# The front of a graph kernel rebuilt: part of VectorE's preparation goes to GpSimd

## The chip, the cores and the metric

The kernel runs on one core of one Trainium2 chip. The metric is the device time of one execution in microseconds. A profile of one execution, with its own time, stands beside the times; times of the trace count from its first instruction.

## The reference, cut to what matters

Two graph layers over 1,250 nodes with 512 features and 21,250 edges. The first is an attention layer, the second a mixture of four expert networks, which this change doesn't touch.

```python
h = jnp.maximum(_layernorm(x), 0.0)
# first layer, nodes = h
h = nodes @ W + b_w
s_dst = h @ a[:D_OUT]; s_src = h @ a[D_OUT:]
e = leaky_relu(s_dst[dst] + s_src[src] + b_a, 0.2)
w = exp(e); alpha = w / segment_sum(w, dst)[dst]
out = segment_sum(alpha[:, None] * h[src], dst)
x = x + out
# second layer: x = x + top-2 mixture of 4 experts, each two mean-aggregating layers
```

## The kernel before, in words

**Front.** The edges come as 170 chunks of 125. TensorE makes, in 22 blocks of up to 8 chunks (`hot_block`, L1811), values that are positive only where an edge's source has the right place within its tile; ScalarE (L794) or VectorE (L1189, block 2 only, `HOT_DVE`) turns them into 0 or 1 while moving them out of PSUM (`hot_columns`). Three pairs of PSUM banks take turns, so block u waits for the eviction of block u - 3. Between the blocks TensorE does small jobs for the table that says which chunks belong to which window of 25 destination nodes (`spread_spans`, `turn_edges`, `sum_tables`, `turn_tables`); VectorE works the table out and signals `tab_ready`. VectorE also takes the statistics of the ten tiles of x (`row_stats`), and ScalarE the square root (`std_ready`); `scales` makes rstd and shift, with which ScalarE normalises tile 0 (`norm`).

**Batches.** Ten batches, b = 0 to 9, each for one tile of 125 nodes and five windows. VectorE makes 25 one-hots for the destinations (L1301). TensorE transposes the normalised tile (L1898), makes 25 counting matmuls (L1860) into CT, then the scores (`scores`, L1879 and L1882, h with the vectors W a) and the product h W (L1923 to L1925). For precision h and W are split in a high and a low part: hT_hi, hT_lo, W0_hi, W0_lo. ScalarE copies high parts (`turned_high0`, `product_high`), the bias into PSUM (`bias_in`) and the counts out (`windows_out`); VectorE makes the low parts (`turned_low0` L1285, `product_low` L1281).

**W and a.** The scores need W a for both halves of a: `source_vectors` (L1184), eight VectorE instructions that multiply 128 x 512 of W with a and sum along the row; two more do the bias (L1260). `first_weights_low` is W0_lo = W - W0_hi (L1270). All of that stands in VectorE's order between batch 0's one-hots and batch 1's. GpSimd (POOL) has made constants and issued three small loads (a_b, bw_b, ba_c) and then waits until the batches are over.

Every engine works through its own list in order, with semaphores between them; in a name of a signal, `x_ready(n)` is a wait for the n-th signal x. `link` makes an engine wait for its own instruction.

## Time and profile before

| | us |
|---|---|
| median of 3 runs | 745.5 (745.43 to 745.51) |
| the profiled execution | 744.08 |
| its span, first to last instruction | 742.3 |
| TensorE busy | 717.8 (97%) |
| VectorE busy | 428.0 (58%) |
| ScalarE busy | 398.1 (54%) |
| GpSimd busy | 184.1 (25%) |

The span is what the trace covers; 1.8 us of the execution's time lie around it. Matmuls are pipelined and their ends are modelled, so busy TensorE is not TensorE at its peak; spans on GpSimd are rough. A group's line gives busy time, the mean of one instruction, and then the idle time before the group.

### The profile page before, as it was taken

Reading aid. Unit: us, or ns where it says so; the run is one execution under the profiler, and the core shown is the slowest. Engines: PE = TensorE matmul, PEld = TensorE weight load, DVE = VectorE, ACT = ScalarE, POOL = GpSimd, SP = SyncE. Lnnn points to the kernel's source line nnn. Section 1 sums busy time; section 2 is a strip of 40 time slices with the busy share of each in tenths; the row PEclk is TensorE's granted clock in tenths of the full one; section 3 lists DMA queues with packets and bytes.
Section 4 is the critical chain, followed back from the end, with each engine's and each line's share of the span. In section 5 each row is a group of like instructions: output and inputs, shape, how many; then the busy total and the mean of one; then the engine's idle time right before and its main releaser. Section 6 shows DMA issues by size and latency. Waiting matters only on the chain.

```text
span 742.3 us, 12047 instructions
## 1 busy us (share of the span) xinstructions
PE 717.8 (97%) x3574; PEld 582.2 (78%) x3574; DVE 428.0 (58%) x1056; ACT 398.1 (54%) x897; POOL 184.1 (25%) x204
## 2 busy tenths in 40 slices
PE   5899999999999999999999999999999999999994
PEld 3589977888888888777777777878888888888883
DVE  8899889999752538622722622657444544444341
ACT  6966769677653521511511511347677667767751
POOL 4000000000000100850300010045666555655511
PEclk9999999999999999999999999999999999999998
DMA  9100000111501247799699695379844994438950
GB/s 207 39 4 3 4 3 18 53 35 35 165 8 58 79 123 240 217 333 326 228 354 328 200 359 197 99 184 264 300 93 88 264 343 120 86 69 225 290 156 6
DMA packets 46444, 115.19 MB, mean 155 GB/s; under 512 B 8340, under 2 KB 8552, under 8 KB 46361
## 3 DMA queue, kind: packets, MB, share of 16 engines
q1 hardware_dynamic: 28581, 77.60, 32.7%
q0 software_dynamic: 9136, 19.65, 11.6%
q10 hardware_dynamic: 8644, 16.86, 6.9%
q8 instruction: 48, 0.79, 0.4%
q14 instruction: 35, 0.29, 0.1%
HBM read 64.89 MB, written 50.08 MB: 155 GB/s over the span
## 4 chain that ended last, share of the span: by engine, by line
PE 92%; DVE 4%; ACT 1%; issue 1%; POOL 0%; DVEq 0%; ACTq 0%; POOLq 0%
PE ps L1783 16%; PE ps L1784 16%; PE ps L1785 16%; PE ps L2185 7%; PE ps L2184 6%; PE ps L2052 3%; PE ps L2053 3%; PE ps L1985 3%; PE ps L1860 3%; PE ps L1979 3%; PE ps L1980 3%; PE ps L2115 2%; PE ps L1923 1%; PE ps L1811 1%; PE ps L1925 1%; PE ps L1924 1%
## 5 line engine op out<-in xcount | busy, mean ns | idle before, releaser
L1110 ACT ACTIVATE agn<-ps,rec 32x128 f32<-32x128 f32 x336 | 120.7, 359 | 38.7 <-PE ps L2185 34.8
L1044 ACT ACTIVATE slots<-he_t 125x512 fp32r<-125x512 f32 x40 | 25.3, 635 | 150.9 <-DVE he_t L1581 146.6
L2185 PE MATMUL ps<-slots,CTs 125*128 x230 | 89.9, 391 | 0.0
L1581 DVE TENSOR_TENSOR he_t<-ps,b_b 125x512 f32<-125x512 f32 x40 | 27.6, 691 | 105.5 <-PE ps L1785 72.3
L728 POOL DMA_INDIRECT hrow<-t_d,piece_i x80 | 76.1, 951 | 25.7 <-issue 23.5
L2184 PE MATMUL ps<-slots,CTs 125*128 x207 | 80.7, 390 | 0.0
L1746 DVE TENSOR_TENSOR tm<-ps,b_b 128x512 f32<-128x512 f32 x23 | 15.9, 692 | 84.3 <-PE ps L1785 84.2
L1783 PE MATMUL ps<-W,agT_hi 128*125 128x512 f32 x160 | 63.5, 397 | 0.0
L1783 PE MATMUL ps<-W,h2T_hi 128*125 128x512 f32 x160 | 63.4, 396 | 0.0
L1785 PE MATMUL ps<-W,agT_lo 128*125 128x512 f32 x160 | 63.3, 396 | 0.0
L1784 PE MATMUL ps<-W,agT_hi 128*125 128x512 f32 x160 | 63.2, 395 | 0.0
L1784 PE MATMUL ps<-W,h2T_hi 128*125 128x512 f32 x160 | 63.2, 395 | 0.0
L1785 PE MATMUL ps<-W,h2T_lo 128*125 128x512 f32 x160 | 63.1, 394 | 0.0
L733 POOL DMA_INDIRECT out<-tg,rec x23 | 37.0, 1607 | 84.2 <-ACT tg L1099 64.3
L1674 DVE CAST CTs<-ps 125x512 fp32r<-125x512 f16 (+1 forms) x69 | 37.3, 596 | 29.1 <-PE ps L2115 29.1
L1301 DVE TENSOR_SCALAR onehot_g<-iota_h,column 125x250 bf16<-125x250 f16 x250 | 49.7, 282 | 5.9 <-PE ps L1860 4.6
L2185 PEld LDWEIGHTS ps<-slots,CTs 125*128 125x128 f32 x230 | 43.2, 188 | 9.7 <-issue 0.3
L2184 PEld LDWEIGHTS ps<-slots,CTs 125*128 125x128 f32 x207 | 38.9, 188 | 8.2
L1979 PE MATMUL ps<-nat_hi,p_hi 125*125 125x512 f32 x100 | 41.0, 410 | 0.2 <-issue 0.2
L712 POOL DMA_INDIRECT crow<-c_d,rec x23 | 22.7, 988 | 73.4 <-DVE W L1549 66.7
L1783 PE MATMUL ps<-slots,heT 128*128 x92 | 38.2, 415 | 1.7 <-DVE heT L1708 1.7
L1980 PE MATMUL ps<-nat_lo,p_hi 125*125 125x512 f32 x100 | 39.5, 395 | 0.0
(316 smaller groups left out, 1665.4 us busy)
## 6 DMA issues: line engine op xcount, KB each, us to landing
he_d<-slots SPq DMA_DIRECT2D x30, 448.0 KB
slots<-he_d SPq DMA_DIRECT2D x30, 448.0 KB
w_d<-slots SPq DMA_DIRECT2D x3, 4096.0 KB, 18.7
slots<-w_d SPq DMA_DIRECT2D x24, 512.0 KB
t_d<-he_t SPq DMA_DIRECT2D x40, 224.0 KB
raw<-in_L_gnn_Wl ACTq DMA_DIRECT2D x4, 1024.0 KB, 7.2
raw<-in_L_gnn_Wr ACTq DMA_DIRECT2D x4, 1024.0 KB, 5.6
slots<-in_L_gnn_Wl ACTq DMA_DIRECT2D x4, 1024.0 KB, 10.0
```

Source lines behind the costliest of these rows:

```text
L728: g.indirect_dma_start(hrow[i % HB][:, q, :], None, t_d.rearrange("e p t (r f) -> (e p t r) f", r=RQ), bass.IndirectOffsetOnAxis(ap=piece_ ...
L733: g.indirect_dma_start(out, bass.IndirectOffsetOnAxis(ap=i32(rec[:, i, 2:3]), axis=0), tg[i % 3][:], None, bounds_check=N - 1, oob_is_err= ...
L1110: last = a.activation(agn[32 * r:32 * r + 32, q, :], ps[n, 3 + i % 2, 128 * r:128 * r + 128], ACT.Copy, scale=rec[n, i, 4:5])
L1301: last = v.tensor_scalar(onehot_g[:, k, j, :], iota_h[:], column[:, b % 2 * BW + k, j:j + 1], None, ALU.is_equal)
L1674: v.tensor_copy(CTs[:, 4 * r:4 * r + n, :], turned_counts(r, n)).then_inc(cts_ready.sem, 1)
L1783: mm(o, l_hi, r_hi, start=start, stop=False)
L1784: mm(o, l_hi, r_lo, start=False, stop=False)
L1785: return mm(o, l_lo, r_hi, start=False, stop=stop)
L1979: mm(o, p_hi[:, g % RA, m, n], nat_hi[:, s, :], start=s == 0, stop=False)
L1980: mm(o, p_hi[:, g % RA, m, n], nat_lo[:, s, :], start=False, stop=False)
L2184: mm(o, CTs[:, t, :], part(k, P, t * 1024, P), start=False, stop=False)
L2185: last = mm(o, CTs[:, t, :], part(k, P, t * 1024 + D, P), start=False, stop=t == T - 1)
```

## The change

- **GpSimd** (after its constants) waits for the small loads and the edge work, adds the two halves of a, multiplies the bias with them and folds the row once (512 to 256). When W has landed it multiplies all of W (128 x 2,048) with each half of a and folds each product once, then makes W0_lo, then folds the nine rows of 256 to 128 and to 64.
- **VectorE** sums the 64 that are left of each row, at the place after hT_lo of batch 0 and ahead of batch 1's one-hots; its own products of W and its W0_lo go. The statistics move behind the table; the registers of batch 0 are loaded during them; `scales` stands after the first five one-hots.
- **ScalarE** makes W0_hi, the bias copy and norm 0 between the last evictions of the front, and the copies of the table's columns later; it waits for wa before it writes nat_hi 0 and the counts of batch 0 (they lie where GpSimd's tiles are).
- **TensorE** makes 12 matmuls of the identity first (`wake`), the hot blocks have all 128 rows (63 of them zero), the small jobs stand one or two blocks later, VectorE evicts block 3 in place of block 2, and batch 0 sums its product by parts: four with both high parts, four with hT_lo, four with W0_lo, and makes the scores last.

```diff
         e_src = at("e_src", [CR, CG, P], F32, 6016)
         e_t = at("e_t", [CR, CG, P], F32, 9024)
         e_g = at("e_g", [CR, CG, P], F32, 12032)
-        e_q = at("e_q", [2 * CR + 1, CG, P], F32R, 15040)
+        e_q = at("e_q", [128, CG, P], F32R, 15040)
         e_mm = at("e_mm", [CR, 2, CG], F32, 18048)
         e_dg = at("e_dg", [CR, 2 * CG, CR], F32, 18112)
...
-        q_sel = at("q_sel", [2 * CR + 1, CR, P], F32R, R1 + 20480)
+        q_row = at("q_row", [128, P], F32, 21920)
+        q_at = at("q_at", [128, CR], F32, 22432)
+        q_sel = at("q_sel", [128, CR, P], F32R, R1 + 20480)
         a_b = at("a_b", [128, 2, D], F32, R1)
-        spill = [at(f"spill_{k}", [128, D], F32, R1 + 6144 + 2048 * k) for k in range(2)]
+        half = D // 2
+        weighed = at("weighed", [128, KC, D], F32, 0)
+        halves = at("halves", [128, 2 * KC + 1, half], F32, 33408)
+        quarters = at("quarters", [128, 2 * KC + 1, half // 2], F32, 33408 + 4 * (2 * KC + 1) * half)
+        eighths = at("eighths", [128, 2 * KC + 1, half // 4], F32, 0)
+        a_sum = at("a_sum", [P, D], F32, R1 + 6144)
+        assert 33408 + 6 * (2 * KC + 1) * half <= R1
         g_b = at("g_b", [NW, NCH], F32, 28704)
...
         SPREAD, SPREAD_BANKS = (4, 4, 2), (5, 7, 5)
         MAGIC = 12582912.0
         WHOLE = NCH // CR
-        HOT_DVE = (2,)
+        HOT_DVE = (3,)
         HOT_ACT = tuple(u for u in range(NU) if u not in HOT_DVE)
...
             for k in range(2):
                 link(g.affine_select(out=q_at[0:2 * CR, :], in_=q_at[0:2 * CR, :], compare_op=ALU.not_equal, fill=1.0,
                                      base=-CR * k, pattern=[[-1, CR]], channel_multiplier=1))
-            link(g.memset(q_at[2 * CR:, :], 1.0))
+            link(g.memset(q_at[2 * CR:2 * CR + 1, :], 1.0))
...
+
+            def folded(o, i, n):
+                return g.tensor_tensor(o, i[:, :, 0:n], i[:, :, n:2 * n], ALU.add)
+
+            pool.wait_ge(*small_in(48))
+            pool.wait_ge(*rows_ready(1))
+            g.memset(halves[:, 2 * KC, :], 0.0)
+            link(g.tensor_tensor(a_sum[:], a_b[0:P, 0, :], a_b[0:P, 1, :], ALU.add))
+            link(g.tensor_tensor(weighed[0:P, 0, :], bw_b[:], a_sum[:], ALU.mult))
+            link(folded(halves[0:P, 2 * KC:, :], weighed[0:P, 0:1, :], half))
+            pool.wait_ge(*w0_in(16))
+            for w in range(2):
+                link(g.tensor_tensor(weighed[:], W0_f[:], a_b[:, w, :].unsqueeze(1).broadcast_to([128, KC, D]), ALU.mult))
+                link(folded(halves[:, w * KC:(w + 1) * KC, :], weighed[:], half))
+            pool.wait_ge(*w0_hi_ready(1))
+            g.tensor_tensor(W0_lo[:], W0_f[:], f32(W0_hi[:]), ALU.subtract).then_inc(w0_lo_ready.sem, 1)
+            link(folded(quarters[:], halves[:], half // 2))
+            folded(eighths[:], quarters[:], half // 4).then_inc(wa_f_ready.sem, 1)
...
             def product_high(t):
                 act.wait_ge(*hw_done(t + 1))
+                if t == 0:
+                    act.wait_ge(*wa_ready(2))
                 copy(nat_hi[:, t, :], ps[0:P, 6, :]).then_inc(hw_hi_ready.sem, 1)
 
             def turned_high0(b):
                 act.wait_ge(*turned(b + 1))
                 if b > 0:
                     act.wait_ge(*hw_done(b))
+                if b == 1:
+                    act.wait_ge(*s_done(1))
                 copy(hT_hi[:], ps[:, 5, 0:KC * P].rearrange("p (c n) -> p c n", n=P)).then_inc(hT_hi_ready.sem, 1)
 
...
             for u in range(NU):
                 if u in HOT_ACT:
                     hot_columns(u)
-                if u == 3:
+                if u == 5:
                     act.wait_ge(*rows_turned(1))
                     copy(e_gc[:], ps[0:P, 7, 0:CG * CR]).then_inc(cols_ready.sem, 1)
-                if u == 10:
+                if u == 13:
                     act.wait_ge(*tab_ready(1))
                     columns(0)
+                if u == 15:
+                    act.wait_ge(*w0_in(16))
+                    copy(W0_hi[:], W0_f[:]).then_inc(w0_hi_ready.sem, 1)
                 if u == 16:
                     act.wait_ge(*var_ready(1))
                     a.activation(std[:], std[:], ACT.Sqrt).then_inc(std_ready.sem, 1)
-            act.wait_ge(*norm_ready(1))
-            norm(0)
-            act.wait_ge(*w0_in(16))
-            copy(W0_hi[:], W0_f[:]).then_inc(w0_hi_ready.sem, 1)
+                if u == 17:
+                    bias_in(0)
+                if u == 18:
+                    act.wait_ge(*norm_ready(1))
+                    norm(0)
 
             for b in range(T):
                 if b == T - 1:
...
-                bias_in(b)
+                if b > 0:
+                    bias_in(b)
+                if b == 0:
+                    act.wait_ge(*wa_ready(2))
                 if b < T - 1:
                     windows_out(b)
 
             link(v.tensor_copy(q_f[:], q_i[:]))
             v.tensor_scalar(q_row[0:CR, :], q_f[0:CR, :], 2.0, None, ALU.mult)
             v.memset(q_row[CR:2 * CR, :], -1.0)
+            v.memset(q_row[2 * CR:, :], 0.0)
             link(v.tensor_tensor(q_f[2 * CR:, :], q_f[2 * CR:, :], q_f[2 * CR:, :], ALU.mult))
-            link(v.tensor_scalar(q_row[2 * CR:, :], q_f[2 * CR:, :], -1.0, 1.0, ALU.mult, ALU.add))
+            link(v.tensor_scalar(q_row[2 * CR:2 * CR + 1, :], q_f[2 * CR:, :], -1.0, 1.0, ALU.mult, ALU.add))
...
+            def batch_flags(b):
+                more = more_here(dve, b)
+                return more, dve.value_load(tab_b[0:1, b:b + 1, BW + 1:BW + 2], min_val=0, max_val=NW * NG)
+
...
-            dve.wait_ge(*x_in(32))
-            row_stats(range(0, 2))
             hot_columns(HOT_DVE[0])
             dve.wait_ge(*spans_spread(1))
...
-            row_stats(range(2, 4))
+            dve.wait_ge(*x_in(32))
+            row_stats(range(0, 1))
             dve.wait_ge(*n_summed(1))
             v.tensor_copy(tab_f[:, 2:3], ps[0:NW, 7, 0:1]).then_inc(tab_f_ready.sem, 1)
-            row_stats(range(4, T // 2))
+            row_stats(range(1, 2))
             dve.wait_ge(*tab_turned(1))
 
...
+            row_stats(range(2, T // 2))
             dve.wait_ge(*x_late_in(32))
-            link(row_stats(range(T // 2, T)))
+            late = row_stats(range(T // 2, T))
+            dve.wait_ge(*flag_ready(2))
+            dve.wait_ge(*tab_ready(1))
+            first_flags = batch_flags(0)
+            link(late)
             for t in range(T):
                 last = v.bn_aggr(x_mv[:, t, :], x_stats[:, t, :])
...
             def sources():
-                dve.wait_ge(*w0_in(16))
-                dve.wait_ge(*small_in(48))
-                source_vectors(0)
-                source_vectors(1)
-                for w in range(2):
-                    dve.wait_ge(*wa_f_ready(2 * KC - 1 + w))
-                    v.scalar_tensor_tensor(spill[w][0:P, :], bw_b[:], 1.0, a_b[0:P, w, :], ALU.mult, ALU.mult,
-                                           accum_out=ab[:, w:w + 1]).then_inc(ab_ready.sem, 1)
-                dve.wait_ge(*wa_f_ready(2 * KC))
+                dve.wait_ge(*wa_f_ready(1))
+                v.tensor_reduce(ab[:, 0:1], eighths[0:P, 2 * KC, :], AX.X, ALU.add).then_inc(ab_ready.sem, 1)
+                link(v.tensor_reduce(wa_f[:].rearrange("p c w -> p w c"),
+                                     eighths[:, 0:2 * KC, :].rearrange("p (w c) n -> p w c n", w=2), AX.X, ALU.add))
                 link(v.tensor_copy(wa[:, :, 0:2], wa_f[:]))
                 v.tensor_tensor(wa[:, :, 2:4], wa_f[:], f32(wa[:, :, 0:2]), ALU.subtract).then_inc(wa_ready.sem, 1)
-                dve.wait_ge(*ab_ready(2))
-                v.tensor_scalar(s_add[:], ab[:, 0:1], ab[:, 1:2], ba_c[:], ALU.add, ALU.add).then_inc(wa_ready.sem, 1)
-
-            def first_weights_low():
-                dve.wait_ge(*w0_hi_ready(1))
-                v.tensor_tensor(W0_lo[:], W0_f[:], f32(W0_hi[:]), ALU.subtract).then_inc(w0_lo_ready.sem, 1)
+                dve.wait_ge(*ab_ready(1))
+                v.tensor_scalar(s_add[:], ab[:, 0:1], ba_c[:], None, ALU.add).then_inc(wa_ready.sem, 1)
 
...
-                more = more_here(dve, b)
-                before = dve.value_load(tab_b[0:1, b:b + 1, BW + 1:BW + 2], min_val=0, max_val=NW * NG)
+                more, before = batch_flags(b) if b > 0 else first_flags
                 dve.wait_ge(*column_ready(b + 1))
                 for k in range(BW):
                     if k == 0:
                         last = v.tensor_scalar(onehot_g[:, k, j, :], iota_h[:], column[:, b % 2 * BW + k, j:j + 1], None,
                                                ALU.is_equal)
                     last.then_inc(step_ready.sem, 1)
+                    if b == 0 and k == 0:
+                        scales()
                 if b == T - 1:
                     turned_low0(b)
                 if b > 0:
                     product_low(b - 1)
-                else:
-                    scales()
-                    sources()
                 if b < T - 1:
                     turned_low0(b)
                 if b == 0:
-                    first_weights_low()
+                    sources()
                 if b == T - 1:
                     source_sums(0, T - 2)
                     spread_out(0)
                                 s_both[:, t:t + n, 0].unsqueeze(2).broadcast_to([P, n, P]), ALU.mult
                                 ).then_inc(sd_ready.sem, 1)
 
-            dve.wait_ge(*flag_ready(2))
...
+            def wake():
+                pe.wait_ge(*consts(2))
+                for _ in range(12):
+                    mm(ps[:, 7, 0:128], ones[:], ident[:], start=True, stop=True)
+
+            wake()
             for u in range(NU):
                 hot_block(u)
-                if u == 2:
+                if u == 3:
                     spread_spans()
-                if u == 3:
+                if u == 4:
                     turn_edges()
-                if u == 7:
+                if u == 9:
                     sum_tables()
-                if u == 8:
+                if u == 10:
                     turn_tables()
-                if u == 9:
+                if u == 11:
                     cover_product()
 
...
-                    pe.wait_ge(*wa_ready(2))
+                    pe.wait_ge(*wa_ready(1))
                 for c in range(KC):
                     first = mm(o, hT_hi[:, c], wa[:, c], start=c == 0, stop=False, skip_group_check=True)
-                    if c == 0:
+                    if c == 0 and b > 0:
                         first.then_inc(batch_done.sem, 1)
                     last = mm(o, hT_lo[:, c], wa[:, c], start=False, stop=c == KC - 1, skip_group_check=True)
                 last.then_inc(s_done.sem, 1)
                 if b == T - 1:
                     pe.wait_ge(*hT_lo_ready(T))
                     spread(0)
-                scores(b)
-                if b == 0:
-                    pe.wait_ge(*w0_lo_ready(1))
+                if b > 0:
+                    scores(b)
                 pe.wait_ge(*bias_ready(b + 1))
                 o = ps[0:P, 6, :]
+                if b == 0:
+                    pe.wait_ge(*hT_hi_ready(1))
+                    for c in range(KC):
+                        first = mm(o, hT_hi[:, c], W0_hi[:, c], start=False, stop=False, skip_group_check=True)
+                        if c == 0:
+                            first.then_inc(batch_done.sem, 1)
+                    pe.wait_ge(*hT_lo_ready(1))
+                    for c in range(KC):
+                        mm(o, hT_lo[:, c], W0_hi[:, c], start=False, stop=False, skip_group_check=True)
+                    pe.wait_ge(*w0_lo_ready(1))
+                    for c in range(KC):
+                        last = mm(o, hT_hi[:, c], W0_lo[:, c], start=False, stop=c == KC - 1, skip_group_check=True)
+                    last.then_inc(hw_done.sem, 1)
+                    scores(0)
+                    return
                 for c in range(KC):
                     mm(o, hT_hi[:, c], W0_hi[:, c], start=False, stop=False, skip_group_check=True)
                     mm(o, hT_hi[:, c], W0_lo[:, c], start=False, stop=False, skip_group_check=True)
```

## Rows read from the trace of the kernel before

**Rows 1.** Cores: the span and the mean granted clock of TensorE.

```profile
core 0: 742.3 us, clock 0.997
```

**Rows 2.** Chain of waits, 24 to 60 us: start us, us, what.

```profile
26.82 0.55 DVEq L396
...
28.23 4.96 DVE onehot_g L1301 x25
...
33.44 4.98 DVE spill L1184 x16
38.42 1.22 DVE spill L1260 x4
...
40.12 0.58 DVE hT_lo L1285
40.70 2.21 DVE W_lo L1270
...
46.00 0.43 PE ps L1898 x4
...
49.13 0.15 PE ps L1879
...
50.05 0.34 PE ps L1923
...
52.94 0.43 PE ps L1898 x4
```

**Rows 3.** Timeline, ScalarE: start us, us, instruction, count.

```profile
25.69 5.45 ACT L794 ACTIVATE onehot_p<-ps 125x1000 bf16<-125x1000 f32 x6
...
35.59 2.00 ACT L770 ACTIVATE W_hi<-W_f 128x2048 fp32r<-128x2048 f32 x1
```

**Rows 4.** Timeline, TensorE matmuls: the counts of batches 0 and 1.

```profile
36.79 4.93 PE L1860 MATMUL ps<-onehot_g,onehot_p 125*125 125x250 bf16 x25
...
46.26 2.87 PE L1860 MATMUL ps<-onehot_g,onehot_p 125*125 125x250 bf16 x25
```

**Rows 5.** Windows: stretch, us, busy us (count) by engine, clock, DMA share, GB/s.

```profile
36.79:41.46 4.67, 4.67 (x27) 4.67 (x25) 4.64 (x15) 3.47 (x9) 0.00 (x0) 1.00 0.03 7
```

**Rows 6.** DMA issues: tile, queue, KB, us from issue to landing.

```profile
W_f<-in_L_gnn_W SPq DMA_DIRECT2D x1, 1024.0 KB, 17.3
...
ba_c<-in_L_gnn_b_a POOLq DMA_DIRECT2D x1, 0.5 KB, 11.3
```

**Rows 7.** Timeline: when those two transfers were issued.

```profile
4.45 0.40 SPq L510 DMA_DIRECT2D W_f<-in_L_gnn_W  x1
...
6.27 0.55 POOL L634 DMA_DIRECT2D ba_c<-in_L_gnn_b_a  x1
```

**Rows 8.** Groups by shape, GpSimd: busy us, mean ns.

```profile
L629 POOL MEMSET e_q<- 1x750 f32 x1 | 0.7, 719 | 0.2 <-POOL ones L627 0.2
...
L644 POOL CAST iota_h<-iota_i 125x250 f16<-125x250 int32 x1 | 0.4, 392 | 0.1
L643 POOL IOTA iota_i<- 125x250 int32 x1 | 0.3, 335 | 0.0
...
L646 POOL CAST wbase<-wbase_i 125x50 f32<-125x50 int32 x1 | 0.2, 226 | 0.1
```

**Rows 9.** One line of GpSimd: duration ns min/median/max, first and last start.

```profile
L708 POOL TENSOR_SCALAR piece_i<-piece_f x4: 583/586/1807, 359.8 to 363.1; 32x92 int32<-32x92 f32 x4
```

**Rows 10.** Timeline, 7.5 to 8.3 us: a VectorE cast and a GpSimd IOTA.

```profile
7.55 0.56 DVE L1169 CAST e_g<-e_i 32x750 f32<-32x750 int32 x1
7.68 0.61 POOL L639 IOTA g_it_i<- 50x170 int32 x1
```

**Rows 11.** Groups by shape, VectorE: 250 elements three ways.

```profile
L1301 DVE TENSOR_SCALAR onehot_g<-iota_h,column 125x250 bf16<-125x250 f16 x250 | 49.7, 282 | 5.9 <-PE ps L1860 4.6 <-issue 1.3
...
L1385 DVE SCALAR_TENSOR_TENSOR z_l<-row,s_rest,row_low 125x250 f32<-125x250 f32 x50 | 21.5, 472 | 0.0
...
L1358 DVE TENSOR_SCALAR row_low<-row 125x250 f32<-125x250 f32 x5 | 1.4, 287 | 1.0 <-ACT row L770 1.0
```

12 lines of the change are left out of this document (2 added, 10 removed).

## The prediction, on record before the changed kernel ran

> **What bounds the kernel now.** I read the cores and their span first: one core, 742.3 us, the granted clock near 1 throughout [rows 1]. The page's slices show TensorE full from the third of forty slices on, so only the first 50 us can hold this change. I then followed the chain of waits through them. From 26.8 to 42.9 us it lies on VectorE: loads of the table's registers, the 25 one-hots of batch 0, eight products of W with a (spill, L1184), two of the bias, W_lo; then TensorE makes batch 0's product, and batch 1 begins at 46.00 and batch 2 at 52.94 [rows 2]. From there each batch follows the last in 6.8 us with TensorE busy, and VectorE goes along with little to spare. So I measure everything by one time: the start of batch 2 on TensorE, 52.94 before. What moves it moves the end.
>
> Two other things to see. ScalarE evicts the one-hot planes without a pause, 0.90 us each (6 in 5.4 us), and has norm 0 and W_hi (2.00) behind them [rows 3]. And TensorE is slow early: the 25 counting matmuls of batch 0 take 4.93 us, those of batch 1 2.87 [rows 4]; 250 columns in 0.20 us is the 1.2 GHz level, in 0.11 us the 2.4 GHz one, though the granted clock is printed as 1.00 in that stretch [rows 5]. Before batch 0 it did mostly matmuls of 65 rows.
>
> **The change part by part.** *Off VectorE* go L1184 (16 entries, 4.98), L1260 (1.22) and W_lo (2.21): 8.4 us of the chain [rows 2]. The register loads ahead of batch 0's one-hots (26.82 to 28.23, 1.4 us) go under the statistics. The statistics move behind the tables, 8 in a row instead of 5, which costs 1.9 us there. In their place VectorE gets one sum of 64 and one of 8 x 64 elements, 0.8 us in all at its one element per cycle.
>
> *ScalarE* does the same work in another order: W_hi, norm 0 and the bias copy now come before the last evictions. Nothing is added; the end of the evictions and the start of batch 0's transposes fall together at about 33.
>
> *TensorE* gets 12 matmuls (fp32, 128 columns) before its first block, when it idles; 63 zero rows per hot block, no time; and it sums W_lo's four matmuls after the eight of W_hi, with the scores last. The whole of a batch (0.43 transposes, 2.7 counts, 0.9 scores from 49.13 to 50.05, 2.8 product) is unchanged [rows 2].
>
> *GpSimd* is where the work goes, and it is the term that decides. It can't start before the last small load: ba_c, issued at 6.27, lands 11.3 later, 17.6. Three instructions (1,280 elements per partition) are done before W lands, at 4.45 + 17.3 = 21.8 [rows 6, 7]. Behind that stand, each waiting for the one ahead: twice (2,048 products, 1,024 sums), W_lo 2,048, then 1,152 and 576 sums. That is 7 instructions and 9,920 elements.
>
> The trace has no two-input instruction on GpSimd, so I bound it. Casts of 50 and 250 elements take 226 and 392 ns: 0.83 ns per element and 0.18 fixed. The memset of 750 takes 719 ns, also 0.8 per element, so a read hides under a write [rows 8]. Lower bound: two reads at once, 0.83 ns. If two reads take turns, 1.66; if the write takes its turn too, 2.5. Upper bound: the tensor_scalar with 92 elements in 583 ns, 4.4 ns [rows 9]. I take 2.1, between "turns" and "all three in turn". Sum: 9,920 x 2.1 = 20.8, 7 x 0.2 for fixed parts and waits = 1.4; end at 21.8 + 22.2 = 44.0.
>
> The page GPSIMD Engine Reference of the Trainium skill (section Performance versus the Vector engine) gives 4,497 ns for an fp32 add of 2,048; no run here shows it yet. By it the 9,920 elements would be 21.8 us and the end about 45, one microsecond later than in my sum.
>
> What is late then: VectorE waits for it in sources(), *ahead of batch 1's one-hots*. Sums, cast, subtraction and s_add 1.3 us (45.3); batch 1's registers are loaded behind them, 1.3 as at 26.82 (46.6); the 25 one-hots 4.96 (51.6); nat_lo and hT_lo, 0.6 each as hT_lo at 40.12 (52.9) [rows 2]. TensorE has stood since its counts: scores 0.9, product 2.8, batch 2 at 56.6. Against 52.94 that is 3.7 us late. ScalarE too waits for wa before windows_out(0), but its 1.4 us end by 48, long before. TensorE's own gain (W_lo at about 40, all counts warm) is lost in this wait.
>
> Each 0.1 ns on the price is 1.0 us. Break-even is an end at 40.3, a price of 1.73 ns. At 0.83 ns GpSimd ends at 31.4 and no longer decides (rival 2); at 4.4 it would end at 67, which the casts give no reason for: that row has strides and a conversion as well.
>
> My forecast: 742.3 + 3.7 in span, 744.08 + 3.7 = 747.8 for the profiled execution, which was 1.4 below the median of 745.5; so 749.2 us, its own range 747 to 752 (prices of 1.9 to 2.4 ns).
>
> **Rivals.**
> 1. *The two engines lock each other out.* The IOTA at 7.68 took 0.61 us for 170 elements, with a VectorE cast (one source, doubled rate) lying over it until 8.11, where 250 elements otherwise take 0.335 [rows 8, 10]; one of the four tensor_scalars took 1,807 ns in place of 583, beside VectorE instructions with two inputs [rows 9]. Batch 0's one-hots are of that kind: 250 elements in 282 ns, where 250 with two tensor inputs take 472 and a one-source one 287 [rows 11]. So one-hots and GpSimd's long instructions would take turns: 25 x 0.2 plus std and shift push GpSimd's end out by about 4.9, to 49, and shift waits up to 4.4 for a product, with norm 0 behind it. Batch 2 at 61.5: 754 us. For it: these rows. Against it: nearly all VectorE instructions beside GpSimd kept their length there, and a short instruction doesn't show how long a long one holds. The page SBUF — State Buffer (section Who interferes with whom) states such a lock, exclusive and for the whole instruction, for these kinds of instruction; by it this rival is the outcome, and the trace agrees for GpSimd as the one that waits.
> 2. *GpSimd is fast enough* (other side). One mechanism: the price per element is under 1.73 ns, and GpSimd ends before VectorE's one-hots need it. The front is then ScalarE's: from 9.6, 20 evictions x 0.90 = 18.0, W_hi 1.9, about 3 for the rest and 0.4 of waits, end at 33; a batch is 6.8; batch 1 at 39.8 in place of 46.0. At up to 1.2 ns it gives 739.5, at 1.5 about 743. For it: one-input instructions run at 0.83 ns. Against it: everything on GpSimd so far seems to move one element per step in each direction.
> 3. *The warm-up does nothing:* TensorE stays at 1.2 GHz through the hot blocks (0.90 per block, as now) and batch 0's counts. Under the forecast this costs nothing, since the counts would end by 41 and GpSimd's end hides them. With a fast GpSimd it leaves batch 1 at about 45: 744.5.
>
> **How the numbers follow.** Forecast 0.33, rival 1 0.27, rival 2 0.27, rival 3 with a fast GpSimd 0.05, and 0.08 for an end within 0.4 us of break-even. About 0.2% (1.5 us) is what a measurement of this kernel tells from no change. So faster by more 0.32, within 0.08, slower 0.60. The range takes in rival 2's 739.5 and reaches past rival 1 to 755; below it and above it I leave about 0.1 each.
>
> **What would show it.** Right: GpSimd's 2,048-element instructions at 4.3 to 4.6 us, its last fold ending at 44 to 45; VectorE idle some 9 us before the 8 x 64 sum, released by GpSimd; batch 1's one-hots not before 46; batch 2 at 56 to 57; batch 0's counts in 2.7. Rival 1: one-hots of several us, norm 0 after 34. Rival 2: products under 3.5 us, VectorE never waiting for GpSimd, batch 1 at 40. Rival 3: counts of 4.9 again. The forecast fails if W lands much earlier, if the price is off by a fifth, or if the one-hots of batch 1 are made ahead of the wait in a way I misread.

## The result and the profile after

The changed kernel takes 755.2 us (median of 4 executions, 753.3 to 760.4) against 745.5 before: a ratio of 1.014, with an interval of 1.0122 to 1.0159. It is slower by more than the forecast of 749.2, and just outside the range that ended at 755.0. The same kernel measured again, on another chip, took 757.8 (753.7 to 761.1) against 745.5, a ratio of 1.0173 (1.0140 to 1.0206). The profiled execution took 753.3 us with a span of 751.6, which stands against 744.08 and 742.3 of before [rows 1].

First GpSimd, on the changed kernel's timeline from 17 to 46 us (start us, us, instruction, count, and in brackets the idle time before it and what ended it):

```profile
17.66 1.28 POOL L662 TENSOR_TENSOR a_sum<-a_b 125x512 f32<-125x512 f32 x1
21.19 4.56 POOL L667 TENSOR_TENSOR weighed<-W_f,a_b 128x2048 f32<-128x2048 f32 x1
25.83 2.35 POOL L657 TENSOR_TENSOR halves<-weighed 128x1024 f32<-128x1024 f32 x1
28.26 4.53 POOL L667 TENSOR_TENSOR weighed<-W_f,a_b 128x2048 f32<-128x2048 f32 x1
32.87 2.39 POOL L657 TENSOR_TENSOR halves<-weighed 128x1024 f32<-128x1024 f32 x1
35.34 4.55 POOL L670 TENSOR_TENSOR W_lo<-W_f,W_hi 128x2048 fp32r<-128x2048 f32 x1
39.85 2.61 POOL L657 TENSOR_TENSOR quarters<-halves 128x1152 f32<-128x1152 f32 x1
42.55 1.47 POOL L657 TENSOR_TENSOR eighths<-quarters 128x576 f32<-128x576 f32 x1
```

2,048 elements take 4.56 us, 2.2 ns each, and the last fold ends at 44.02. The prediction had 2.1 ns and 44.0. Two small misses cancel there: the chain began at 21.19 and not at 21.8, and took 22.83 us and not 22.2. These are the two-input rows that the trace of before lacked; the 4,497 ns of the page GPSIMD Engine Reference of the Trainium skill (section Performance versus the Vector engine) agrees with them to 1.4%.

Now VectorE, the same view from 25 to 57 us:

```profile
25.91 2.30 DVE L1280 TENSOR_SCALAR std<-x_mv 125x10 f32<-125x10 f32 x1
28.13 7.42 DVE L1327 TENSOR_SCALAR onehot_g<-iota_h,column 125x250 bf16<-125x250 f16 x5
35.46 0.20 DVE L1285 RECIPROCAL rstd<-std 125x10 f32<-125x10 f32 x1
35.70 4.22 DVE L1286 SCALAR_TENSOR_TENSOR shift<-x_mv,rstd 125x10 f32<-125x10 f32 x1
39.84 7.57 DVE L1327 TENSOR_SCALAR onehot_g<-iota_h,column 125x250 bf16<-125x250 f16 x20
47.32 0.67 DVE L1312 TENSOR_TENSOR hT_lo<-ps,hT_hi 128x500 fp32r<-128x500 f32 x1
48.04 0.68 DVE L1292 TENSOR_REDUCE wa_f<-eighths 128x8 f32<-128x512 f32 x1
50.75 4.97 DVE L1327 TENSOR_SCALAR onehot_g<-iota_h,column 125x250 bf16<-125x250 f16 x25 [1.50 <-issue]
55.63 0.69 DVE L1308 TENSOR_TENSOR nat_lo<-ps,nat_hi 125x512 fp32r<-125x512 f32 x1
```

shift writes ten elements and takes 4.22 us; 25 one-hots that took 4.96 before [rows 2] take 15.0. The ends show why. std ends at 28.21, GpSimd's fold at 28.18; shift ends at 39.92, GpSimd's W_lo at 39.89. The one-hots as the view by tile of onehot_g has them, from 25 to 46 us (ns: shortest, median, longest):

```profile
L1327 DVE TENSOR_SCALAR onehot_g<-iota_h,column x19: 276/277/4551, 28.1 to 46.0; 125x250 bf16<-125x250 f16 x19
```

Most keep their 277 ns; the longest is held for 4,551, the length of a whole GpSimd instruction. Taken one by one, four are held, for 4.55, 2.36, 2.71 and 1.43 us, and each ends within 0.1 us of the end of a GpSimd instruction (the second product, its fold, and the last two folds). One or two short ones pass between two such waits. VectorE never waits for GpSimd's *result*: when it comes to the sums at 47.91 the last fold is 3.9 us old. What follows on the other engines, on the timelines of ScalarE and TensorE:

```profile
39.95 0.81 ACT L835 ACTIVATE h_f<-xs,shift,rstd 125x512 f32<-125x512 f32 x1 [9.19 <-DVE shift L1286]
42.87 1.09 PE L1928 MATMUL ps<-ident,h_f 125*128 125x125 f32 x4 [11.48 <-ACT onehot_p L818]
43.76 4.81 PE L1890 MATMUL ps<-onehot_g,onehot_p 125*125 125x250 bf16 x25
52.29 0.65 PE L1928 MATMUL ps<-ident,h_f 125*128 125x125 f32 x4
60.71 0.59 PE L1928 MATMUL ps<-ident,h_f 125*128 125x125 f32 x4
```

Norm 0 waits 9.19 us for shift, TensorE 11.48 for the evictions behind norm 0, and batch 2 starts at 60.71. On the same timeline of before it starts at 52.78 (the chain, which lists what TensorE was released by, has it 0.16 later [rows 2]). I compare timelines from here on: +7.93 us.

TensorE's clock, from the view by windows (us, busy us and count of PE, PEld, DVE, ACT, POOL, then the granted clock, DMA share, GB/s):

```profile
18.00:23.00 5.00, 4.29 (x20) 1.95 (x18) 4.58 (x16) 5.00 (x8) 4.76 (x4) 1.00 0.38 136
23.00:36.00 13.00, 5.01 (x11) 2.11 (x11) 12.90 (x22) 7.76 (x13) 12.69 (x5) 0.62 0.00 1
26.00:27.00 1.00, 0.43 (x2) 0.00 (x0) 1.00 (x1) 1.00 (x1) 1.00 (x1) 0.58 0.00 0
36.00:46.00 10.00, 3.13 (x14) 2.84 (x15) 10.00 (x15) 4.78 (x11) 7.93 (x3) 0.50 0.01 2
52.00:62.00 10.00, 9.66 (x65) 8.29 (x66) 10.00 (x48) 5.78 (x16) 0.00 (x0) 1.00 0.02 4
```

The twelve matmuls did their work early (the hot blocks ran at the 2.4 GHz level up to 23 us), but TensorE then had little to do: behind a gap of 1.07 us that ended at 24.75 and a few more matmuls it fell back to 1.2 GHz between 26 and 27 us. Batch 0's counts took 4.81 us, much as before [rows 4].

Not all of the loss is here. The profiled execution lost 753.30 - 744.08 = 9.22 us; 7.93 of it by batch 2. The rest arises at one place at about 500 us, on the chain of waits:

```profile
494.02 0.69 ACT agn L1139
494.70 5.63 another core or an unknown queue
500.36 0.60 ACT aggT L794
500.98 0.69 DVE aggT L1755
```

The 5.63 us are not all loss: before the same copy, at 491.16, ScalarE of before waits 4.22 us as well, for TensorE. Up to 488 us the same instructions stand 7.8 us later than in before, behind this wait 9.2: it costs 1.4.

### The profile page after: what moved, and what is told of

It reads as the page before. It is cut to its first block, busy times and chain, and to the rows that moved or that the text cites. A ratio compares the mean times of both kernels' runs of the same rounds, so it can differ in the third digit from the quotient of the medians.

```text
span 751.6 us, 12092 instructions
## 1 busy us (share of the span) xinstructions
PE 717.2 (95%) x3598; PEld 581.1 (77%) x3598; DVE 436.6 (58%) x1038; ACT 398.3 (53%) x897; POOL 209.6 (28%) x215
## 4 chain that ended last, share of the span: by engine, by line
PE 90%; DVE 5%; ACT 2%; issue 1%; another core or an unknown queue 1%; DVEq 0%; POOL 0%; ACTq 0%; POOLq 0%
PE ps L1807 16%; PE ps L1808 16%; PE ps L1809 16%; PE ps L2229 7%; PE ps L2228 6%; PE ps L2029 3%; PE ps L2023 3%; PE ps L2096 3%; PE ps L2097 3%; PE ps L2024 3%; DVE onehot_g L1327 3%; PE ps L1890 3%; PE ps L2159 2%; PE ps L1967 1%; PE ps L1969 1%
## 5 line engine op out<-in xcount | busy, mean ns | idle before, releaser
L1327 DVE TENSOR_SCALAR onehot_g<-iota_h,column 125x250 bf16<-125x250 f16 x250 | 59.7, 323 | 6.1 <-PE ps L1890 4.6
```

The source lines that it names most:

```text
L1327: last = v.tensor_scalar(onehot_g[:, k, j, :], iota_h[:], column[:, b % 2 * BW + k, j:j + 1], None, ALU.is_equal)
```

## The experiments

Two numbers are given for each: the time, and the start of batch 2 on TensorE's timeline (52.78 before, 60.71 in the changed kernel), which measures the front alone.

**The changed kernel once more.**

> The changed kernel once more, unedited, to see how its front and its later part vary from one execution to the next. Expected: one-hots lengthened by the same GpSimd instructions, batch 2 on TensorE at 60.9 again, and the spread of several us, if it is there again, in the part after 480 us.

757.8 us, ratio 1.0173 (1.0140 to 1.0206), batch 2 at 61.01. The front repeats within 0.3 us; the time of an execution does not: 753.7, 757.1, 758.5, 761.1, where nearly all of 19 executions of before on that chip lay between 744.8 and 746.9, and one at 748.0.

**GpSimd's work left out.** This run leaves out W's products, the sums of the bias and W_lo, which is set to zero; the rest of the change stays.

```
-            link(g.tensor_tensor(a_sum[:], a_b[0:P, 0, :], a_b[0:P, 1, :], ALU.add))
...
-            folded(eighths[:], quarters[:], half // 4).then_inc(wa_f_ready.sem, 1)
+            g.memset(eighths[:], 0.0).then_inc(wa_f_ready.sem, 1)
```

> GpSimd's work is left out of the changed kernel: W's low part and the folded products are set to zero by two memsets, done before 19 us; all else stays. Theory (GpSimd and VectorE shut each other out for whole instructions, and GpSimd's chain ends at 44): with both gone std takes 0.17 us in place of 2.3, the five first one-hots 1.1 us in place of 7.4, shift 0.17 in place of 4.22; norm 0 at 30, evictions over at 33, batch 0's counts at the 2.4 GHz pace (2.7 us), batch 2 on TensorE at 46.5 to 47.5 against 60.87: about 739.5 us. Rival (the reordering itself, for instance the later statistics or the small jobs of TensorE, costs part of the loss): batch 2 later than 50.

744.2 (740.8 to 745.7), ratio 0.9996 (0.9983 to 1.0009), batch 2 at 49.61. shift is back to 0.17 us, the one-hots to 0.2 each, norm 0 starts at 30.47, the transposes at 33.50. So GpSimd's presence costs 60.71 - 49.61 = 11.1 us of front, and the rest of the change gains 3.2, half of what I had expected (batch 2 at 46.5 to 47.5). The chain of waits of this run from 33 us says where the other half went:

```profile
33.50 1.10 PE ps L1915 x4
34.60 4.76 PE ps L1877 x25
42.90 0.51 PE ps L1915 x4
43.41 2.71 PE ps L1877 x25
```

Batch 0's transposes and counts are on the path and at 1.2 GHz: 5.86 us against batch 1's 3.22, so 2.6 us by this chain. The granted clock was 0.58 from 23 to 36 us.

**The same work in pieces of 256 elements,** so that GpSimd's instructions last 0.6 to 1.0 us each.

```
+                for c in range(KC):
+                    for h in range(2):
+                        n = slice(h * half, (h + 1) * half)
+                        last = g.tensor_tensor(weighed[:, c, n], W0_f[:, c, n], a_b[:, w, n], ALU.mult)
```

> The same sums on GpSimd, but cut: each 2,048-element instruction as eight of 256, each fold of 1,024 as four of 256, the last two folds as three each. Theory (a VectorE instruction waits for the GpSimd instruction that has the port, at most one): no one-hot waits longer than about 0.7 us, the 25 take turns with the pieces; std takes at most 0.8, shift at most 0.8, norm 0 starts at about 31 instead of 39.95 and the one-hots end at 42 or earlier instead of 47.4. GpSimd has 24 instructions more, of which each costs some 0.1 us, and waits for one-hots in between: its end at 47 to 51 instead of 44.0. Batch 2 then at 59 to 63. Rival (the wait is for the whole chain, whatever the pieces): one-hots of several us again. Rival (no exclusion, only GpSimd's length counts): its end at 46 to 47, no longer.

756.9 (755.9 to 757.6), ratio 1.0177 (1.0160 to 1.0194), batch 2 at 61.18. VectorE's timeline of this run:

```profile
25.96 2.97 DVE L1341 TENSOR_SCALAR onehot_g<-iota_h,column 125x250 bf16<-125x250 f16 x5
29.09 0.48 DVE L1300 SCALAR_TENSOR_TENSOR shift<-x_mv,rstd 125x10 f32<-125x10 f32 x1
29.49 12.23 DVE L1341 TENSOR_SCALAR onehot_g<-iota_h,column 125x250 bf16<-125x250 f16 x20
48.37 0.22 DVE L1305 TENSOR_REDUCE ab<-eighths 125x1 f32<-125x64 f32 x1 [6.07 <-POOL eighths L657]
```

The wait of one VectorE instruction shrinks with GpSimd's (shift 0.48 for 4.22), and norm 0 is at 30.50. The one-hots still take 15.2 us together, in more and shorter waits, but with std and shift hardly held VectorE is through with them at 41.64, 5.7 us sooner than in the changed kernel. What eats this gain is GpSimd: 38 instructions for 7 put its end at 48.3. VectorE then does wait for the result, 6.07 us. Batch 2 lies in the 59 to 63 that I had expected.

**Scales out of the way.** std, its reciprocal and the operand of shift lie in PSUM, and the scales go ahead of all one-hots; so norm 0 can't be held.

```
-                v.scalar_tensor_tensor(shift[:], x_mv[:, :, 0], -1.0, rstd[:], ALU.mult, ALU.mult
+                v.scalar_tensor_tensor(shift[:], x_mv[:, :, 0], -1.0, ps[0:P, 7, 416:416 + T], ALU.mult, ALU.mult
```

> Of the changed kernel, std, rstd and shift keep one operand in PSUM, so that no VectorE instruction of theirs has two tensor inputs in SBUF or is a one-source one wholly in SBUF, and they stand ahead of batch 0's one-hots. Theory: std in 0.2 us at 26, shift in 0.2 us beside a running GpSimd instruction, norm 0 at 29 to 30 in place of 39.95, evictions over by 33. The one-hots still take turns with GpSimd and end at 47, so batch 2 stays at 60 to 61 and the time within 1 us of the changed kernel; the 4.2 us of shift were cover for nothing but themselves. Rival (it is norm 0's lateness that costs the time): batch 2 at 54 or earlier. Rival (VectorE waits for GpSimd whatever its operands): shift takes several us again.

757.0 (752.5 to 759.2), ratio 1.0162 (1.0121 to 1.0203), batch 2 at 60.98. shift takes 0.17 at 28.83 beside GpSimd's 4.53, norm 0 is at 30.47, the transposes at 33.50. The 25 one-hots take 18.7 us, to 47.7, and batch 2 is where it was. So ScalarE's 9.19 and TensorE's 11.48 of waiting cost nothing by themselves; the one-hots do.

**The one-hots of batch 0 from PSUM as well.** The ramp iota_h is copied into PSUM once and read from there.

```
+                        last = v.tensor_scalar(onehot_g[:, k, j, :], ps[0:P, 7, 160:160 + WT] if b == 0 else iota_h[:], column...
```

> As the one before, and batch 0's 25 one-hots read the column numbers as fp32 from PSUM, at one element per cycle. Theory: each takes 0.4 us (spacing about 0.38) whatever GpSimd does, all 25 are done at 39, hT_lo before 40, and GpSimd's chain ends at 44.0 as before. What is left of the loss is then what the prediction had: the sums at 44 to 45.5, batch 1's one-hots at 46.8, batch 2 on TensorE at 56.6, about 749 us. Rival (contention has another cause than the operands of the one-hots, such as a limit of SBUF as a whole): one-hots of several us in spite of PSUM, batch 2 at 60 or later.

748.9 (748.1 to 753.7), ratio 1.0072 (1.0056 to 1.0089), batch 2 at 57.03. VectorE's timeline of this run:

```profile
28.92 9.73 DVE L1331 TENSOR_SCALAR onehot_g<-ps,column 125x250 bf16<-125x250 f32 x25
44.23 0.22 DVE L1293 TENSOR_REDUCE ab<-eighths 125x1 f32<-125x64 f32 x1 [5.00 <-POOL eighths L657]
47.08 4.96 DVE L1331 TENSOR_SCALAR onehot_g<-iota_h,column 125x250 bf16<-125x250 f16 x25 [1.51 <-issue]
```

With a PSUM source a one-hot takes 0.39 us in place of 0.20 and none is held, though GpSimd is busy throughout. What is left is the forecast, step by step: end of GpSimd 44.20 (44.0), batch 1's one-hots 47.08 (46.6), batch 2 57.03 (56.6). The time of 748.9 us beside the forecast's 749.2 is in part luck: it stands against 744.0 of before on that chip, not 745.5, so the whole is 4.9 us longer where the forecast had 3.7, and the profiled execution of this version took 753.7. The front says more: without the lock the change still costs 4.25 us of it. The other 7.4 down to the 49.61 of the run without GpSimd's work go with the wait for its result.

**The clock alone.** The kernel before with only the twelve matmuls and the 128 rows.

```
+            for _ in range(12):
+                mm(ps[:, 7, 0:128], ones[:], ident[:], start=True, stop=True)
...
-        e_q = at("e_q", [2 * CR + 1, CG, P], F32R, 15040)
+        e_q = at("e_q", [128, CG, P], F32R, 15040)
```

> The kernel before with two parts of the change alone: the 12 matmuls ahead of the first block and the hot blocks with all 128 rows. Theory: TensorE runs its hot blocks at the 2.4 GHz pace (0.45 us in place of 0.9), but VectorE's chain (one-hots, W times a, W_lo) sets batch 1 at 46.0 all the same; only what stood ahead of the tables gets shorter, by 0.5 to 2 us, and moves that chain as a whole: 743.5 to 745.5. Rival (the warm-up carries over to batch 0's counts and that is what was missing): batch 0's counts in 2.7 us and a gain of 2 us or more.

747.9 (743.8 to 752.6), ratio 1.0032 (1.0002 to 1.0061), batch 2 at 51.10. The warm-up is worth 1.7 us of front, as the expectation had it, and the kernel is not faster: at 747.9 it lies outside the expected 743.5 to 745.5. From 24.85 to 31.6 us the blocks have the pace of the changed kernel, one in 0.89 us, but no gap of over 0.3 us between them, and the level holds:

```profile
24.00:31.00 7.00, 5.01 (x14) 2.05 (x14) 5.60 (x35) 7.00 (x10) 0.00 (x0) 1.00 0.00 0
```

It had been lost once before, behind a gap of 1.88 us that ended at 18.07 (0.55 from 20 to 23.7 us), and is lost again in the gap of 2.47 us ahead of the transposes (0.50 from 34 to 36 us); batch 0's counts take 3.88.

**W's products and low part back on VectorE,** GpSimd keeping only the bias.

```
-                link(g.tensor_tensor(weighed[:], W0_f[:], a_b[:, w, :].unsqueeze(1).broadcast_to([128, KC, D]), ALU.mult))
...
+                    v.scalar_tensor_tensor(to, W0_f[:, c, :], 1.0, a_b[:, w, :], ALU.mult, ALU.mult,
+                                           accum_out=wa_f[:, c, w:w + 1]).then_inc(wa_f_ready.sem, 1)
...
+                    v.tensor_tensor(W0_lo[:], W0_f[:], f32(W0_hi[:]), ALU.subtract).then_inc(w0_lo_ready.sem, 1)
```

> The changed kernel with W's products and W_lo back on VectorE (eight products that sum along the row, 5.0 us, and 2.3), placed around hT_lo of batch 0; GpSimd keeps only the bias, which it has done by 21 us, ahead of W. Everything else of the change stays. Theory: nothing shuts VectorE out, its list runs from 26 to hT_lo of batch 1 without a stop: 5.0 + 0.4 + 2.5 + 0.6 + 2.3 + 2.5 + 0.5 + 1 + 5.0 + 1.3 = 21, so hT_lo of batch 1 at 47 and batch 2 on TensorE at 50.5 to 51: 743 us, 2 us better than before. Rival (the reordered front costs as much as it gives): 745.5 or more.

747.6 (743.8 to 753.4), ratio 1.0020 (0.9993 to 1.0046), batch 2 at 52.55. Nothing is held, the one-hots take 0.2 each, and the front is that of before within 0.23 us. I had expected batch 2 at 50.5 to 51 and 743 us; the rival (745.5 or more, the reordered front costs what it gives) holds.

Three of these kernels have a front that is earlier than before's and none is faster by more than can be measured. The last five runs are about the other loss and about TensorE's clock.

**Twelve matmuls of one column** ahead of the first hot block, in the kernel before; nothing else.

```
+            for _ in range(12):
+                mm(ps[:, 7, 0:1], ones[:], ident[:, 0:1], start=True, stop=True)
```

> The kernel before with twelve matmuls of a single column ahead of the first hot block, where TensorE is idle until 9.0 us: they give TensorE almost no work, so its clock and the front stay as they were, and only the instructions behind them stand twelve matmuls further on in TensorE's program. In the runs so far the offset of batch 2 does not carry over to the whole: one run of this study with only twelve matmuls and 128 rows had batch 2 1.7 us earlier and a whole 2.4 us longer, and every changed kernel lost 1 to 4 us more than its front did, between 485 and 560 us, in waits of VectorE or ScalarE that no semaphore of another engine explains. Theory A (these losses come with where the later code lies or when it is fetched, and any change ahead shifts it): the front is unmoved, and the whole is 1 to 4 us longer than 745.5, with a spread of several us over the executions. Theory B (they come from the shift in time, that is from what the layer-2 phase meets in the queues when it begins earlier or later): with the front unmoved the whole is 745.5 within 0.5 us and as steady as before.

744.0 (743.9 to 748.9), ratio 1.0019 (1.0003 to 1.0036), batch 2 at 52.79, before's within 0.01. The eleven executions fall in two groups: seven from 743.9 to 745.2, four from 748.2 to 748.9. Beside them 27 of before lay from 743.9 to 745.5. So theory A holds for four executions in eleven; the median is before's. The profiled one is of the second group. Its VectorE timeline near 495 us, and TensorE's, whose transposes VectorE copies:

```profile
494.99 0.68 DVE L1674 CAST CTs<-ps 125x512 fp32r<-125x512 f16 x1
499.71 1.02 DVE L1674 CAST CTs<-ps 125x512 fp32r<-125x512 f16 x2 [4.05 <-remote]
493.55 0.74 PE L2118 MATMUL ps<-ident_h,crow 128*125 128x128 f16 x10
```

In before the three copies stand together:

```profile
494.81 1.61 DVE L1674 CAST CTs<-ps 125x512 fp32r<-125x512 f16 x3
```

Between the first copy and the second the program has one wait, for transposes that ended at 494.3 by this timeline; VectorE stands for 4.05 us more. "remote" says that a signal did come just then and that the view can't match it to the end of an instruction. The packed trace has the time of every signal. The three of these transposes (`crow_turned`) came at 493.77, 494.01 and 494.12 in before, each 0.02 us or less behind its transpose; here they came at 494.04, 499.69 and 499.76, for transposes that end at 493.94, 494.17 and 494.29. So VectorE waited for TensorE's signal, which came 5.5 us late.

What follows on TensorE: it works on until 505.1, then stands 2.25 us for VectorE, and behind this gap it falls to the 1.2 GHz level for three microseconds, which costs another 1.6 us (from the view by windows):

```profile
505.00:507.30 2.30, 0.07 (x2) 0.00 (x0) 2.24 (x6) 1.35 (x2) 0.00 (x0) 1.00 1.03 237
508.40:511.40 3.00, 3.00 (x8) 2.31 (x7) 2.97 (x7) 2.90 (x9) 2.39 (x3) 0.50 1.01 244
```

**The clock alone with twelve one-column matmuls more,** behind its own twelve.

```
             for _ in range(12):
                 mm(ps[:, 7, 0:128], ones[:], ident[:], start=True, stop=True)
+            for _ in range(12):
+                mm(ps[:, 7, 0:1], ones[:], ident[:, 0:1], start=True, stop=True)
```

> The run with twelve matmuls and 128 rows, and twelve matmuls of a single column more. The front should begin batch 2 at 51.3 as that run did, 1.7 us ahead of before. Theory A (where the code lies): the whole differs from that run's 747.9, by 1 us or more, since the code lies elsewhere while the times are the same. Theory B (the shift in time): the same whole, 747.9 within its spread.

744.7 (743.6 to 746.3), ratio 1.0009 (1.0000 to 1.0018), batch 2 at 52.52. The added matmuls held back the first hot block by 1.5 us (10.46 for 9.01), which I had not reckoned with, so the front's gain fell to 0.3. The whole, though, is shorter against before than in the run without them, and its spread is 2.7 us in place of 8.8. That doesn't decide between the theories: the front moved too, and the two runs were on different chips, on one of which before itself ranged over 3.2 us (744.8 to 748.0) and on the other over 1.6.

**TensorE kept at work.** The version with W on VectorE, with two to five small matmuls ahead of each hot block from the twelfth on and behind the last.

```
+            def fill(u, n):
+                for _ in range(n):
+                    mm(ps[:, u % 3 * 2, 0:128], ones[:], ident[:], start=True, stop=True)
...
+                if u > 11:
+                    fill(u, 4 if u in (16, 18, 19) else 2)
```

> The version that gives VectorE W's products and low part back, with small matmuls (two to five, in the PSUM bank that the next block overwrites) ahead of each hot block from the twelfth on and behind the last, so that TensorE does not stand idle between 23 and 33 us. Theory (the 1.2 GHz level in 23 to 36 us costs the rebuilt front its gain): the granted clock stays at 1.00 up to the counts, batch 0's counts take 2.9 us in place of 4.7, batch 1's begin about 2 us sooner and batch 2 comes at about 50 where it came at 52.7; if nothing is given back later the whole is about 743 to 745. Rival (VectorE or ScalarE sets the front there whatever TensorE's clock): batch 2 stays at 52.7 within 0.5 us.

744.8 (744.7 to 745.2), ratio 1.0010 (1.0001 to 1.0019), batch 2 at 53.61. The windows of this run have the clock where it should be:

```profile
23.00:27.00 4.00, 3.82 (x29) 3.08 (x27) 3.89 (x19) 4.00 (x9) 0.00 (x0) 1.00 0.01 4
27.00:31.00 4.00, 2.93 (x20) 2.20 (x18) 3.62 (x20) 4.00 (x7) 0.00 (x0) 1.00 0.01 2
34.00:39.00 5.00, 5.00 (x40) 4.54 (x39) 3.61 (x6) 2.35 (x7) 0.00 (x0) 1.00 0.00 0
```

Batch 0's counts take 3.76 us for 4.66. It buys nothing: here VectorE (W_lo and the second four products behind hT_lo) sets the front, as the rival had it, and the fillers made the transposes 1.6 us later (35.04 for 33.47), which is more than the 1.1 us that batch 2 lost (53.61 for 52.55, so not within the rival's 0.5 either). It is the steadiest of all versions, with 0.5 us between its eleven executions.

**Twenty-four one-column matmuls in the kernel before,** and then twelve in the changed kernel, behind its own.

```
+            for _ in range(24):
+                mm(ps[:, 7, 0:1], ones[:], ident[:, 0:1], start=True, stop=True)
```

> The kernel before with twenty-four matmuls of one column ahead of the first hot block, where the last run had twelve. That run's executions fell in two groups, 743.9 to 745.2 (seven) and 748.2 to 748.9 (four), with the kernel before at 743.9 to 745.5 beside it, and its profiled execution, of the second group, stood 4.05 us in VectorE between the first and the second copy of turned counts near 500 us, with TensorE's transposes long done. Theory (what a wait for instructions costs there depends on where the code lies): the fastest executions are again at 743.9, since the front is unmoved, and the share and size of the slow group differ from the last run's, perhaps to none. Rival (more instructions ahead, more loss): the slow group grows, and the median goes to 748 or more.

749.8 (749.1 to 750.5), ratio 1.0058 (1.0045 to 1.0072), batch 2 at 57.19. The expectation fell with its premise: TensorE's timeline shows that these matmuls are not small.

```profile
3.18 10.40 PE L1846 MATMUL ps<-ident,ones 128*128 128x1 f32 x48 [3.18 <-POOLq L628]
13.44 2.01 PE L1811 MATMUL ps<-q_sel,e_q 65*125 65x500 f32 x4
```

Each matmul has two entries. 48 entries in 10.4 us are 0.22 each for one column, against 0.20 for one of 128 (24 in 4.87). TensorE's weight loads (PEld) are busy for 10.3 of these 10.4 us, so the weights' load sets the time. Behind the twelve matmuls of the clock's run, 24 one-column entries took 2.74 us, 0.11 each: here too TensorE was at the 1.2 GHz level, though the clock is printed as 1.00 in this stretch. The first hot block went from 9.0 to 13.4, and 4.41 of the 5.36 us that the profiled execution lost is this.

> The changed kernel with twelve matmuls of one column behind its own twelve: nothing else differs. In all runs so far the fastest execution of a kernel was the kernel before's time plus the offset of batch 2 in the trace (changed kernel: 745.5 + 7.9 = 753.4, measured 753.3; the run without GpSimd 744.0 - 3.2 = 740.8, measured 740.8), and the rest of its executions 0 to 8 us above. Theory (the front loses 7.9 us, the rest is the late waits, which depend on where the code lies): the fastest execution is 744.0 + 7.9 to 8.2, that is 751.9 to 752.3 on a chip where before is 744.0, or 753.4 to 753.7 where it is 745.5, and the median lies another distance above it than in the two looks at the changed kernel (1.9 and 4.1 us). Rival (the extra over the front's loss belongs to the changed front itself): the same median as before, 755 to 758.

754.2 (752.9 to 756.0), ratio 1.0115 (1.0096 to 1.0133), batch 2 at 63.03. Neither side of the expectation can be read from it, since the front moved by 2.3 us. But how it moved is of use. The VectorE timeline of this run:

```profile
31.90 1.48 DVE L1280 TENSOR_SCALAR std<-x_mv 125x10 f32<-125x10 f32 x1
33.30 9.77 DVE L1327 TENSOR_SCALAR onehot_g<-iota_h,column 125x250 bf16<-125x250 f16 x5
44.40 3.98 DVE L1327 TENSOR_SCALAR onehot_g<-iota_h,column 125x250 bf16<-125x250 f16 x20
```

A later start met GpSimd's instructions in another order. The last instruction of VectorE's table, ten elements (`tab_b`, L1267), was held for 3.91 us at 22.41 by the first product, where it took 0.34 at 19.98 in the changed kernel; five one-hots then took 9.8 us while the twenty behind GpSimd's last instruction took 0.2 each.

All profiled executions side by side: the front's part (batch 2 against 52.78), and what is left of the whole against 744.08.

| kernel | profiled us | by batch 2 | after it | executions, us |
|---|---|---|---|---|
| changed | 753.30 | +7.93 | +1.29 | 753.3 to 760.4 |
| changed, once more | 753.69 | +8.23 | +1.38 | 753.7 to 761.1 |
| no GpSimd work | 740.81 | -3.17 | -0.10 | 740.8 to 745.7 |
| pieces | 755.85 | +8.40 | +3.37 | 755.9 to 757.6 |
| scales in PSUM | 757.77 | +8.20 | +5.49 | 752.5 to 759.2 |
| one-hots in PSUM | 753.66 | +4.25 | +5.33 | 748.1 to 753.7 |
| clock alone | 743.81 | -1.68 | +1.41 | 743.8 to 752.6 |
| W on VectorE | 748.91 | -0.23 | +5.06 | 743.8 to 753.4 |
| twelve short | 748.32 | +0.01 | +4.23 | 743.9 to 748.9 |
| clock, twelve short | 743.83 | -0.26 | +0.01 | 743.6 to 746.3 |
| W on VectorE, kept at work | 745.21 | +0.83 | +0.30 | 744.7 to 745.2 |
| twenty-four short | 749.44 | +4.41 | +0.95 | 749.1 to 750.5 |
| changed, twelve short | 755.62 | +10.25 | +1.29 | 752.9 to 756.0 |

## Why the prediction was wrong

**GpSimd's own term was right.** 9,920 elements at 2.1 ns to an end of 44.0; measured 2.2 ns and 44.02, as close as that only because two misses of 0.6 us cancel. Rival 2, a fast GpSimd, fell with the first product.

**The step that failed is the cost of VectorE's own work beside GpSimd.** The forecast let batch 0's one-hots, std and shift keep their lengths (4.96 us for 25) and made VectorE wait for GpSimd's end. Rival 1 had the mechanism, and it is what happened: the one-hots took 15.0 us, shift 4.22, std 2.30. Leaving GpSimd's work out brought batch 2 from 60.71 to 49.61; leaving all of it in and only taking the VectorE operands to PSUM brought it to 57.03, near the forecast's own 56.6. The page SBUF — State Buffer (section Who interferes with whom) of the Trainium skill, cited under rival 1, states the exclusive lock; this trace agrees, with 4.22 us for ten elements.

**Rival 1 had the wrong engine wait.** It pushed GpSimd's end to 49 and held shift for up to 4.4. GpSimd lost next to nothing: its three instructions of 2,048 elements took 4.53 to 4.56 (4.51 to 4.55 in the version with the one-hots from PSUM), the seven together 22.83 us (22.73), and its end was 44.02. VectorE paid in each exchange, while in [rows 9, 10] it was GpSimd that was held. The time from 28.1 to 47.3 that its 25 one-hots and shift need contains all of what GpSimd has to do from 28.3 to 44.0, and then 17 one-hots at full pace. The sum came out alike (batch 2 at 60.71 against 61.5) and the place differs: the forecast's wait for the sums is gone, swallowed by the longer one-hots, and it comes back as soon as the lock is removed: 4.25 us of front, with VectorE 5.00 us idle for GpSimd.

**I gave the rival too little.** 0.27 against 0.33 for the forecast, though the rows for it [rows 9, 10] were exceptions that nothing else explained (1,807 ns for 583, 0.61 for 0.335). The case against it, that VectorE's instructions beside GpSimd kept their length, rested on GpSimd's one-input instructions, most of them under 1 us. And the range ended 1 us above the rival's 754, less than the rival's own uncertainty.

**TensorE's clock: the warm-up was half right.** It did run the hot blocks up to 23 us at 2.4 GHz and is worth 1.7 us alone. "All counts warm" was wrong: ScalarE's evictions pace the blocks (two matmuls of 500 columns, by estimate 0.44 us at the 0.11 per 250 of [rows 4], in each 0.90). That alone did not lose the level, as the clock alone shows; the changed kernel has two longer gaps (1.07 and 1.92 us) besides, and it was lost behind the first. Batch 0's counts, where nothing held them up, took 4.45 to 5.0 in every version but the clock alone (3.88) and the one that filled the gaps (3.76). Rival 3 put this outcome on the warm-up doing nothing; the level was reached and given up. In the run without GpSimd's work the lower level costs 2.6 us by the chain, which is why the front gained 3.2 where the 39.8 for batch 1 of rival 2 would have given 6.

**The term that was missing.** The prediction had everything behind batch 2 move as one. Up to 480 us it does: the distance to before changes by less than 0.3 us in every version. The table's fourth column has -0.1 to +5.5 us, all of it behind that point, in layer 2. That such a loss can arise without any change of the front is shown (twelve short matmuls: 0.01 by batch 2, 4.23 after it, in four of eleven executions, and in none of 27 of before beside them). Before has smaller ones of its own: on the chip where the clock alone was measured its 19 executions range from 744.8 to 748.0.

In seven of the thirteen rows the fastest execution is 744.08 plus the front's part within 0.3 us (no GpSimd work, scales in PSUM, one-hots in PSUM, both with W on VectorE, twelve short, clock with twelve short); for the changed kernel it is 1.3 above, at 753.3 for 752.0. But 744.08 is a single execution. Beside the changed kernel the fastest of before was 745.43, and 745.43 + 7.93 is 753.4. So of the 9.7 us between the medians 7.9 are the front, and 1.9 are the distance of the changed kernel's median from its own fastest execution; the rest is rounding and before's own spread. One row has no such sum: the changed kernel with twelve short matmuls has its fastest execution at 752.9, where 744.08 + 10.25 is 754.3, so its front can't be the same in every execution.

**What stays open** is why these signals are late. The thirteen versions have 59 waits of over 1 us in VectorE or ScalarE that the views call remote, and before has none. Each of the 59 ends with a signal of TensorE, 1.5 to 7.1 us behind the end that the timeline gives the last TensorE instruction that raises it (1.6 at the wait of the changed kernel near 500 us). Not every one costs time: the clock with twelve short matmuls has two. As the ends on TensorE's timeline are modelled, it can't be said whether the signals came late or the matmuls did. Loads of the program's own code are in the records too, as 16 KB packets of an instruction queue. In the run with twelve short matmuls none was under way while VectorE stood still: one ended at 485.0, and the next began at 500.17, half a microsecond after VectorE had gone on. Its row in the view of the DMA queues from 500 to 501.5 us (packets, MB, share of 16 engines):

```profile
q8 instruction: 1, 0.02, 5.2%
```

The page Runtime: NRT & Kernel Launch of the Trainium skill (section Instruction fetch mechanics) says that engines stream their instructions in blocks through a DMA queue of their own, and that crossing a block costs little unless a branch leaves the window. No run here shows a load as the cause, and in this run the packets speak against it; of the 59 waits 41 have no such packet in them. That twelve matmuls ahead can bring a wait of 4 us is shown on one chip (four of eleven executions against none of 27); the way from the one to the other is not.

No version that does all of the work beats the kernel before by more than the measurement can tell. The nearest are the one with W on VectorE and TensorE kept at work (1.0010) and the clock with twelve short matmuls (1.0009).

## What to carry to other kernels

Before work is moved to GpSimd, list what VectorE does in the same stretch. Here std, shift and the one-hots, with SBUF operands, were held for whole GpSimd instructions, however short they are (bn_stats was not: 0.66 us beside a product), so the price of the move was GpSimd's duration on VectorE's clock. If it must be, give VectorE's instructions a PSUM operand, and compare: 0.39 us for 0.20 a one-hot was worth 4 us here. Cutting GpSimd's work let VectorE go 5.7 us sooner here, but GpSimd ended 4.3 us later and VectorE then waited 6.07 us for the result. And see that GpSimd's end comes before it is needed even without the lock: here 7.4 of the 11.1 us went with that wait. And where a front is a few microseconds of a long kernel, measure it by a landmark behind it besides the whole: here the whole moved by up to 5.5 us for reasons that lay 430 us later.
